# Four clears in one place instead of three spread between the gathers and scatters of a decoder kernel

## The reference

```
x = ln(x + L0_attn(x));  x = ln(x + L0_xattn(ctx, x));  x = ln(x + L0_ffn(x))
x = ln(x + L1_attn(x));  x = ln(x + L1_xattn(x, ctx));  x = ln(x + L1_ffn(x))
```

## Time and profile before

| | before |
|---|---|
| median of three runs | 1628.96 us (1628.24 to 1632.61) |
| the profiled execution | 1632.61 us |
| its span, first to last instruction | 1630.8 us |
| POOL busy | 726.8 us, 45% of the span |
| PE busy | 1381.1 us, 85% |
| DVE, ACT busy | 1132.0 and 936.3 us, 69% and 57% |
| indirect DMAs of line 1020 and of line 1084 | 64 and 64 |
| clears, line 1011 | 96, 53.3 us |
| mean granted TensorE clock | 0.939 of full speed |

### The profile page before, as it was taken

The page is one execution under the profiler, slowest core; times in us unless marked ns, Lnnn a source line. Parts: engine busy times, 40 slices in busy tenths (PEclk is TensorE's granted clock), DMA queues, the critical chain, the costliest instruction groups (busy, mean ns, idle before and its releaser), DMA issues.

```text
span 1630.8 us, 47453 instructions
## 1 busy us (share of the span) xinstructions
PE 1381.1 (85%) x19192; PEld 1120.0 (69%) x19192; DVE 1132.0 (69%) x3503; ACT 936.3 (57%) x2474; POOL 726.8 (45%) x1072
## 2 busy tenths in 40 slices
PE   6899999999988998889988899988999973999900
PEld 4788788788765776666776677766677752788800
DVE  3777877877766667788677887767876764455465
ACT  3455556655533687745877548785568951444411
POOL 5514434424225216556245752447542253354465
PEclk8799999999998999999999999999999996999955
DMA  9942112111121001100010110001000001677543
GB/s 328 384 140 76 63 63 78 57 66 50 50 78 27 15 9 28 32 25 28 9 28 25 32 34 9 25 22 35 26 20 12 15 25 49 219 222 229 171 141 97
DMA packets 112635, 124.06 MB, mean 76 GB/s; under 512 B 22048, under 2 KB 85536, under 8 KB 112160
## 3 DMA queue, kind: packets, MB, share of 16 engines
q1 hardware_dynamic: 105760, 107.26, 20.9%
q0 software_dynamic: 6656, 13.78, 2.6%
HBM read 65.72 MB, written 55.28 MB: 74 GB/s over the span
## 4 chain that ended last, share of the span: by engine, by line
PE 53%; DVE 21%; ACT 9%; POOL 8%; issue 5%; DMA 1%; another core or an unknown queue 1%; SPq 0%; DVEq 0%; POOLq 0%; ACTq 0%
PE bank L1956 5%; PE bank L1823 5%; PE bank L2203 4%; PE bank L2210 4%; PE bank L1808 3%; ACT P L1234 3%; PE bank L2078 3%; PE bank L2043 3%; PE bank L1835 3%; POOL rows_x L1084 2%; PE bank L2004 2%; PE bank L2000 2%; PE bank L1993 2%; DVE P L1588 2%; PE bank L1923 2%
## 5 line engine op out<-in xcount | busy, mean ns | idle before, releaser
L1823 PE MATMUL bank<-const,P 128*128 128x128 f32 x1152 | 174.5, 283 | 14.6 <-ACT P L1234 6.3
L1823 PEld LDWEIGHTS bank<-const,P 128*128 128x128 f32 x1152 | 132.0, 144 | 48.7 <-ACT P L1234 15.6
L1234 ACT ACTIVATE P<-bank,gs 128x128 f32<-128x128 f32 x512 | 142.7, 393 | 32.1 <-DVE gs L1577 30.8
L1956 PE MATMUL bank<-XT,wb 128*128 128x256 f32 x512 | 144.9, 405 | 7.7 <-ACT PT L1139 4.3
L1041 POOL TENSOR_TENSOR P<-P,gs 128x512 f32<-128x512 f32 x64 | 66.6, 1047 | 152.5 <-DVE gs L1624 152.0
L1242 ACT ACTIVATE PT<-bank 128x512 f32<-128x512 f32 x192 | 110.7, 615 | 35.8 <-PE bank L1823 35.0
L1094 POOL DMA_INDIRECT y_rows<-R,gidx x80 | 76.6, 957 | 96.7 <-DVE R L1763 82.3
L1587 DVE TENSOR_REDUCE gs<-bank 128x8 f32<-128x512 f32 x128 | 87.3, 682 | 42.1 <-PE bank L1808 29.5
L1577 DVE TENSOR_REDUCE gs<-bank 128x4 f32<-128x512 f32 x128 | 83.0, 685 | 43.7 <-PE bank L2078 43.4
L1956 PEld LDWEIGHTS bank<-XT,wb 128*128 128x128 f32 x512 | 89.5, 195 | 25.5 <-ACT PT L1139 8.7
L954 POOL TENSOR_SCALAR rstd<-mv 128x2 f32<-128x2 f32 x80 | 18.4, 230 | 185.2 <-DVE mv L1365 184.4
(11 more groups left out here) (286 smaller groups left out, 3792.5 us busy)
## 6 DMA issues: line engine op xcount, KB each, us to landing
Q<-in_wm SPq DMA_DIRECT2D x40, 578.5 KB
rows_x<-blank SPq DMA_DIRECT2D x4, 5016.0 KB, 37.7
y_mid<-PT SPq DMA_DIRECT2D x16, 512.0 KB, 2.9
y_mid<-D SPq DMA_DIRECT2D x16, 512.0 KB, 2.8
XW<-rows_x SPq DMA_DIRECT2D x40, 132.0 KB
wb<-in_wb SPq DMA_DIRECT2D x1, 4228.0 KB, 15.0
V<-in_ctxT SPq DMA_DIRECT2D x32, 128.0 KB, 2.7
P<-y_rows SPq DMA_DIRECT2D x32, 128.0 KB, 2.4
```

The source lines that it names most:

```text
L1234: ins = act.activation(P[s][:, i, 128 * g:128 * g + 128], banks[s][i][:, 128 * g:128 * g + 128], ACT.Exp, bias=gs[s][:, 0, 4 * i + g:4 * i ...
L1823: last = pe.transpose(tile(banks[s][i], t), tile(P[s][:, i, :], t), ident)
L1956: mm(half(s, 2 * (e % 2) + k), tile(B("gu"), 2 * e + k), XT[s][:, :], start=True, stop=True).then_inc(a_up_ps.of(s), 1)
```

## The change

In both loops the order becomes: for each t, first four clears in a row if t is not 0, then the two DMAs of k = 0 and 1 with nothing between them. A group so has 4 clears in one place instead of 3 in three places, and the kernel 128 instead of 96.

```diff
             def clear_again():
-                pool2(pool, pool.memset(blank[:, :], 0.0))
+                for _ in range(4):
+                    pool2(pool, pool.memset(blank[:, :], 0.0))

             def fetch(n, s):
 ...
                 for t in range(T):
+                    if t:
+                        clear_again()
                     for k in range(2):
-                        if t or k:
-                            clear_again()
                         pool.indirect_dma_start(y_two[s][:, k, 128 * t:128 * t + 128], ...)
 ...
                 for t in range(T):
+                    if t:
+                        clear_again()
                     for k in range(2):
-                        if t or k:
-                            clear_again()
                         pool.indirect_dma_start(d["rows_x"][:, :], ...)
```

## The result

The changed kernel took 1652.57 us (median of four, 1649.35 to 1654.88), the kernel before 1628.60 us on the same chip. The ratio is 1.0152, with a 95% interval from 1.0135 to 1.0169: 24 us slower, where 12 were forecast. The time lies above the range, which ended at 1650.

What follows compares the result with a forecast made beforehand. The second stage's chain of waits through POOL was taken as the bound: 13 of 32 groups on it at 0.85 us give 11.1 us, the others 1 us, so 1628.96 becomes 1641.1 us; range 1633 to 1650 us.

Steps and rivals of the forecast that it cites:

- The place and the sign: Second stage gets longer, third and fourth are only shifted; 83% for slower, 12% the same, 5% faster.
- The cost of a group: POOL's gather and scatter groups: each 1.91 - 1.06 = 0.85 us longer, from 0.40 to 1.45 at the bounds.
- The pair: Two DMAs of one t, k = 0 and 1, with no clear between: starts 1.26 us apart instead of 1.79.
- the sum: Second stage: 11.1 us from groups on the chain plus 1 us from the others, 1641.1 us against the median.
- Groups on the chain and off it: Second stage's 32 groups: 13 on the chain of waits delay the end in full, 19 off it add about 1 us.
- the 13: Three gather and ten scatter groups on the second stage's chain of waits: 13 x 0.85 = 11.1 us.
- the 19: Second stage's groups off the chain of waits: delay can be absorbed by idle times, 1 us put on them, at most 9.
- The clear within a pair: Clear between the DMAs of k = 0 and 1: removing two of them saves 1.06 us of POOL's time per group.
- All groups count: Rival, all 32 groups: delays off the chain add up at 0.85 us each, 27 us, 1656 us; 8%.
- Only the ends count: Rival, second stage: only three gather groups at its start and two scatter groups at its end cost, 4.3 us; 14%.
- The gap between clears: Rival, POOL's run of clears: a gap other than 0.08 us makes the 13 groups cost 5 or 19 us; 10%.
- It gets faster: Rival, POOL: the hand-over from clear to DMA stalls, and 64 of 96 go; about 1623 us with thirteen stalls; 6%.

Runs made afterwards that it cites:

- 0, 3, 0: Against the kernel before: three clears between t = 0 and 1, none between k = 0 and 1; 0.9986 and 1.0009 on quicker chips, 1.0084 on a slower one.
- 1, 2, 1: Against the kernel before: two clears between t = 0 and 1, one between each k = 0 and 1; 1.0106 on a quicker chip, 1.0069 on a slower one.
- 0, 4, 0: The changed kernel against the kernel before: four clears between t = 0 and 1, none within pairs; 1.0152 and 1.0126 on slower chips, 1.0089 and 1.0103 on quicker.

## Why the prediction was wrong, step by step

**The place and the sign** were right: the second stage carries the loss, and the last stages are only shifted (253.9 and 253.6 us).

**The cost of a group** was 0.72 instead of 0.85 us, within the bounds. The pair was right to 0.02 us. Four clears take 2.34 us where the sum had 4 x 0.555 + 3 x 0.08 = 2.46.

**Groups on the chain and off it.** The step was "a longer piece on the chain moves the end by its full length", with 11.1 us for the 13 and "1 us as an estimate" for the 19. The runs show 7.8 (4.8 to 10.7) and 6.5 us (4.2 to 8.6), on the quick chip. The first can still be the full length of the smaller group, 13 x 0.72 = 9.4, but that chip's chain need not be the one that I had read. The second is what failed: 19 places off the chain cost 6.5 us together, where the sum had an estimate of 1. Which of them had too little slack isn't shown. The two errors nearly cancel, and the sum of 12 us stands against 14 to 17 on the quick chips.

**The clear within a pair.** This step made the forecast wrong. It ran "two of the three clears go. [...] That saves 1.06 us per group": I had priced the clear by POOL's time alone, and the distance between the DMAs at nothing. I had looked at what close DMAs do to POOL (the earlier trace rows in stage three), not at what they do to PE. On the slow-fed chips, to which that of the forecast belongs, PE's trains of small matmuls stall beside indirect DMAs, and more so the closer these stand. The five runs of 0, 3, 0 and 1, 2, 1 show its price: 0, 3, 0 costs 13.7 us there and nothing on quick chips, and 0, 4, 0 (1.0126 and 1.0152) costs 9 to 14 us more than 1, 2, 1 (1.0069), where on quick chips the two are the same. Added to the 14 us of the quick chips, the 13.7 would make 28; 20.5 and 24 were measured, so the two parts don't add in full, or the chips of this kind differ.
The row that would have warned me stood in the trace of before: 10.7 us of idle time on PE with no releaser, nearly all of it within 2 us behind the start of an indirect DMA. It was the ninth part of PE's waits in that stage and I passed over it, as it was no wait for POOL. A second sign stood in the earlier trace rows, "another core or an unknown queue 1%", on a program of one core. All eight profiles from slow-fed chips have that share of 1 or 2%, and none of the twelve from quick chips.

**The rivals.** "All groups count" gave 1656 us on a mechanism that the runs bear out in part: groups off the chain do cost, though 0.34 of the 0.72 us that was added, and not in full. "Only the ends count" fell: the gathers at the start cost at most 1.9 us on a quick chip, and the loss is spread over groups on and off the chain. "The gap between clears" had bounds that held, and the gap, 0.06 us, was near the 0.08 of the sum. "It gets faster" rested on one stall and fell. No rival had PE in it.

**What stays open.** What holds up PE isn't shown, nor what holds up the releases that DVE and ACT wait for. PE's idle time has no releaser in the profile, and I have not tried whether the instructions, the semaphores, the records of the profiler or something else is late; it isn't the profiler alone, since the times taken without a profile differ in the same way. Why one chip shows it and another not is open too. No profile of the kernel before was taken on a quick chip, so its idle time there isn't known. The kinds of chip were told by the kernel before and by PE's unnamed idle time, on six sets of runs in all.

## What to carry to other kernels

An instruction that only passes time on one engine can set the distance between transfers; before it is moved, look at what the other engines do in the microseconds behind each transfer, not only at its own queue. Idle time with no releaser is worth a row by line and by what runs beside it, even where it is small, since a change can multiply it; so is a share of the chain that goes to an unknown sender. The chain of waits gives the length of what is on it, but many places off the chain can together cost nearly as much; and where a result is to hold for more than one chip, time it on more than one.

## What the runs showed of the hardware

- Indirect DMAs from GpSimd 1.26 us apart stalled TensorE's trains of small matmuls on some chips: 32 matmuls in 4.0 us instead of 0.63, in goes of 2 to 16 with 0.3 to 0.5 us between. At 1.79 us apart the same stage lost 10 us to such idle time instead of 37.
- On the same chips VectorE and ScalarE waited for releases whose sender the profile doesn't name: 43 us in the second stage with the DMAs of a group 1.25 to 1.41 us apart, none in that stage of the kernel before with them 1.79 us apart, and none on the quick chips in any form.
- One and the same kernel was 2.9% slower than another on one chip and 1.6 to 1.7% faster than it on another, in two sets. The kernel before took 1615 us on two chips, and 1627 to 1631 on two others.
- A fill of 128 x 528 floats on GpSimd took 0.54 us and one of 128 x 8 took 0.10, with 0.06 us between two that wait for one another. An indirect DMA starts 0.30 us behind the end of another, and 0.28 behind a fill that it waits for.
